# A warm-up of 128 instead of 256 rows, the sum of squares on VectorE and the cast of the scan on ScalarE, in an eight-core layer

## The chip, the cores and the metric

The kernel runs on the 8 cores of one Trainium2 chip (two dies of four cores). The metric is the device time of the slowest core in microseconds. Engine names in what follows: PE is TensorE, ACT is ScalarE, DVE is VectorE, POOL is GpSimd, SP is SyncE, which here only issues transfers.

## What is computed

```python
xn = _layernorm(x, axis=-1)                       # x: (4, 4096, 2048)
x = x + _L0_attn_ref(xn, ...) + _L0_ffn_ref(xn, ...)

# _L0_attn_ref
xp = jnp.einsum('btd,ed->bte', x, W_in)
dt = jax.nn.softplus(jnp.einsum('btd,hd->bth', xp, W_dt) + b_dt)
a = jnp.exp(dt[..., None] * A_cont)               # A_cont = -exp(log_A)
ys[t] = a[t] * ys[t - 1] + xh[t]                  # written as an associative scan
y = jnp.einsum('btd,ed->bte', ys.reshape(Bsz, Tlen, D), W_out)

# _L0_ffn_ref: weights int8, 2048 -> 8192 -> 2048
gate = jax.nn.silu(_qmatmul(x, w_gate, s_gate))
up = _qmatmul(x, w_up, s_up)
return _qmatmul(gate * up, w_down, s_down)
```

## The kernel before, in words

Each core takes 2048 consecutive rows of x (half a sequence of one batch). The scan would need the state of the rows before; instead every core begins WU = 256 rows early (zeros for the first half of a sequence) and lets the state decay in. So T = 2304 rows, 18 tiles of 128, are normalised and projected, and 2048 are put out. The rows are also cut into chunks of 512, 512, 512, 512 and 256 (CH_OFF, CH_LEN).

Nothing is scheduled by a planner: each engine and each queue runs its instructions in the order in which the Python emits them, and semaphores tie them together.

Start-up. emit_wc_step(r), 16 times, folds W_dt into W_in: a 1 MB piece of W_in is loaded by POOL (L219, cast to bf16 in the transfer), 16 matmuls of 32 columns (L226), an ACT copy (L231). Between the steps stand the first ten emit_ln_front and the first eight emit_ln_back.

emit_ln_front(tile): ACT issues the load of one x tile of 128x2048 f32 into one of three buffers xtb (L253), waits for it and squares it with a running sum (L259); DVE sums the tile (L265) and makes the small statistics (L267 to L274). emit_ln_back(tile): ACT takes the inverse root by Ln and Exp (L284, L287), the shift (L290), and writes the normalised tile in bf16 to xnb (L294); SP sends it to the scratch xn_scr (L300). From the fourth tile on, xnb is written only when the write of three tiles back has landed.

emit_tr(chunk): SP waits until all writes to xn_scr emitted so far have landed and issues 16 transposing transfers into xnT, 128x(chunk length) each (L317). emit_dtl(chunk): 16 matmuls give the dt logits of the chunk (L330), five ACT steps make the softplus (L337 to L346), three DVE steps split it in two bf16 parts (L348 to L354).

emit_m1_et(pass, et), one group for each of 16 feature tiles in each of two passes. Pass 0 covers chunks 0 and 1 (1024 columns), pass 1 chunks 2, 3 and 4 (1280 columns). In a group: the selector matmuls spread dt over the partitions (L402, L405), ACT takes the exponential into ab (L410), the projection takes 16 matmuls for each chunk (L424), ACT copies the result from PSUM to xpsb (L439), the DVE scan runs over the pass's columns (L451). Then emit_cast_spill of the group before: DVE casts the scan's result to bf16 (L470) and POOL writes it to ys_scr (L478). ab, xpsb, ysb and ybfb have two buffers each; the selector banks of pass 0 have one each.

In pass 0 the remaining tiles are normalised between the groups (dicts fr for fronts, bk for backs), and chunks 2, 3 and 4 are transposed behind groups 4, 8 and 10, their dt logits behind groups 5, 9 and 11:

```python
bk = {0: 8, 1: 9, 2: 10, 3: 11, 4: 12, 5: 13, 6: 14, 7: 15, 8: 16, 9: 17}
```

After pass 1 the feed-forward part runs: 64 steps of 128 matmuls of 512 columns (L611, gate and up), then four blocks of the down and output projections (L722, L728) with the residual added (L736). Its first loads wait until all of ys_scr is written.

Of the kernel before, what the change touches and what calls it, by code (L numbers as in the profile page):

```python
# [17 lines left out]
P = 128  # L18
# [4 lines left out]
WU = 256  # L23
# [3 lines left out]
CH_LEN = (512, 512, 512, 512, 256)  # L27
# [47 lines left out]
def build_nc():  # L75
# [24 lines left out]
    with contextlib.ExitStack() as top:  # L100
# [69 lines left out]
        xps_b = [AE(nc.sbuf_tensor(f"xpsb{i}", [P, 1280], F32)) for i in range(2)]  # L170
# [4 lines left out]
        a_b = [AE(nc.sbuf_tensor(f"ab{i}", [P, 1280], F32)) for i in range(2)]  # L175
# [3 lines left out]
        ys_b = [AE(nc.sbuf_tensor(f"ysb{i}", [P, 1280], F32)) for i in range(2)]  # L179
        ybf_b = [AE(nc.sbuf_tensor(f"ybfb{i}", [P, 1280], BF16)) for i in range(2)]  # L180
# [55 lines left out]
        PASS_LEN = (1024, 1280)  # L236
# [8 lines left out]
        def emit_ln_front():  # L245
# [10 lines left out]
            r_dx.wait(AC, kb)  # L256
            if i >= 3:
                AC.wait_ge(c_xn.h, i - 2)
            achain(AC.activation(out=xsq_s[:, :], in_=xt_b[kb][:, :], func=AF.Square,  # L259
                                 accum_out=stats[:, cb + 1:cb + 2]))  # L260
            sq_done = e_act.n
# [4 lines left out]
            VE.wait_ge(e_act.h, sq_done)  # L266
# [195 lines left out]
        def emit_cast_spill(p_of, gi2):  # L462
            k2 = gi2 % 2
            pln = PASS_LEN[0] if gi2 < NE else PASS_LEN[1]
            p2 = 0 if gi2 < NE else 1
            et2 = gi2 % NE
            VE.wait_ge(c_scan.h, gi2 + 1)
            if gi2 >= 2:
                VE.wait_ge(r_dys.h[k2], r_dys.cnt[k2])
            inst = VE.tensor_copy(out=ybf_b[k2][:, 0:pln], in_=ys_b[k2][:, 0:pln])  # L470
            c_ybf.inc(inst)
            GP.wait_ge(c_ybf.h, c_ybf.n)
            if p2 == 0:
                tt0, nblk, col0 = 0, 6, WU
            else:
                tt0, nblk, col0 = 6, 10, 0
            r_dys.refill(GP, k2)
            r_dys.inc(GP.dma_start(out=ys_scr[tt0:tt0 + nblk, :, et2, :]  # L478
                                   .rearrange("t p c -> p t c"),
                                   in_=ybf_b[k2][:, col0:col0 + nblk * P]  # L480
                                   .rearrange("p (t c) -> p t c", c=P)), k2)
# [17 lines left out]
        fr = {0: 1, 1: 1, 2: 1, 3: 1, 4: 1, 5: 1, 6: 1, 7: 1}  # L499
        bk = {0: 8, 1: 9, 2: 10, 3: 11, 4: 12, 5: 13, 6: 14, 7: 15, 8: 16, 9: 17}  # L500
# [326 lines left out]
```

## Time and profile before

| | us |
|---|---|
| median of 2 runs (3606.3 and 3607.96) | 3607.13 |
| the profiled execution | 3609.48 |
| its span, on core 0, the slowest | 3607.9 |
| span of core 3, the fastest | 3580.5 |
| spans of cores 1, 2, 4, 5, 6, 7 | 3584.4, 3592.2, 3601.9, 3592.8, 3606.7, 3589.5 |
| PE busy on core 0 | 3242.1 (90%) |
| DVE, ACT, POOL busy | 463.3, 537.8, 223.0 |
| mean granted TensorE clock on core 0 | 0.967 |

The span is the time from the first to the last instruction of one core; the profiled execution's own time includes a little around it. Busy times add up over stages that have different limits, so a stage is read from its own stretch: which engine works without a gap, what the others wait for, and what the chain of waits (the work followed back from the last instruction) passes through. The granted clock is TensorE's, 1.0 being 2.4 GHz and 0.5 being 1.2 GHz. A line with SPq or ACTq is a transfer's issue on that engine's queue.

### The profile page before, as it was taken

To read this page: it belongs to the slowest core of one execution; us is meant where nothing else is said; L and a number is where in the kernel's file an instruction comes from. 1 tells how busy PE (TensorE), PEld (TensorE's weight loads), DVE (VectorE), ACT (ScalarE), POOL (GpSimd) and SP (SyncE) were. 2 spreads that over 40 slices of the span, in tenths; PEclk is the share of its full clock that TensorE was granted. 3 is DMA by queue.
4 is the path that set the end of the run, shared out by engine and by line. 5 is a ranking of instruction groups with operands and counts; after the bars stand their busy time and mean duration, and the time that the engine had idled before them with its cause. 6 is when DMAs were issued, how large, how long until landed. Compare 5 with 4: busy or idle time off the path is not lost.

```text
span 3607.9 us, 36929 instructions; the slowest of 8 cores (3580.5 to 3607.9 us)
## 1 busy us (share of the span) xinstructions
PE 3242.1 (90%) x15088; PEld 1460.5 (40%) x15088; DVE 463.3 (13%) x540; ACT 537.8 (15%) x776; POOL 223.0 (6%) x318
## 2 busy tenths in 40 slices
PE   0164897999999999999999999979998997997999
PEld 0021343444444444444444444434433443443444
DVE  1132232000000000000000002200013004003000
ACT  2243222111211111112211111100000000000000
POOL 1000111000001000100010001000000000000000
PEclk9887898999999999999999999989999999998999
DMA  8755443112111211221121113256456547546443
GB/s 184 140 146 118 85 84 94 53 53 71 53 53 56 68 53 53 59 65 53 53 67 57 53 53 106 88 139 223 177 213 217 180 175 252 183 175 233 175 175 114
DMA packets 126758, 419.03 MB, mean 116 GB/s; under 512 B 51248, under 2 KB 51264, under 8 KB 111488
## 3 DMA queue, kind: packets, MB, share of 16 engines
q0 software_dynamic: 44544, 176.52, 18.9%
q1 hardware_dynamic: 79456, 221.28, 18.2%
q10 hardware_dynamic: 2592, 18.88, 1.7%
q8 instruction: 122, 2.00, 0.2%
q14 instruction: 44, 0.36, 0.0%
HBM read 322.38 MB, written 68.16 MB: 108 GB/s over the span
## 4 chain that ended last, share of the span: by engine, by line
PE 85%; DMA 8%; SPq 2%; ACT 2%; issue 1%; DVE 1%; POOL 0%; ACTq 0%; DVEq 0%; POOLq 0%
PE ps_g L611 25%; PE ps_u L611 25%; PE pso L728 24%; PE pso L722 6%; PE ps_xp L424 5%; DMA xtb<-x_full 4%; SPq L317 2%; DMA wdq_sb<-wd 2%; DVE wdq_sb L550 1%; ACT xsq_s L259 1%; DMA xn_scr<-xnb 1%; DMA ftb<-f_scr 0%; PE psdtl L330 0%; ACT ab L410 0%; PE psdtl L402 0%
## 5 line engine op out<-in xcount | busy, mean ns | idle before, releaser
L728 PE MATMUL pso<-wdq_sb,ftb 128*128 128x512 bf16 x4096 | 920.2, 385 | 61.6 <-DVE wdq_sb L550 61.6
L611 PE MATMUL ps_g<-xnT,wgb 128*128 128x512 bf16 x4096 | 897.4, 380 | 17.4 <-DMA wgb<-wg 17.4
L611 PE MATMUL ps_u<-xnT,wub 128*128 128x512 bf16 x4096 | 894.5, 379 | 0.0
L728 PEld LDWEIGHTS pso<-wdq_sb,ftb 128*128 128x128 bf16 x4096 | 403.2, 99 | 567.8 <-issue 99.5
L611 PEld LDWEIGHTS ps_g<-xnT,wgb 128*128 128x128 bf16 x4096 | 400.7, 98 | 503.5 <-issue 21.5
L611 PEld LDWEIGHTS ps_u<-xnT,wub 128*128 128x128 bf16 x4096 | 401.4, 98 | 482.6
L634 DVE TENSOR_TENSOR fb<-gb,ub 128x512 bf16<-128x512 bf16 x256 | 108.8, 425 | 1565.8 <-ACT ub L626 1565.8
L626 ACT ACTIVATE ub<-ps_u,su_c 128x512 bf16<-128x512 f32 x256 | 175.9, 687 | 708.2 <-PE ps_u L611 708.2
L623 ACT ACTIVATE gb<-ps_g,sg_c 128x512 bf16<-128x512 f32 x256 | 175.9, 687 | 704.2 <-PE ps_g L611 704.2
L424 PE MATMUL ps_xp<-xnT,winTb 128*128 128x512 bf16 (+1 forms) x1280 | 265.2, 368 | 0.0
L722 PE MATMUL pso<-wo_sb,ytb 128*128 128x512 bf16 x1024 | 233.5, 381 | 26.1 <-DMA ftb<-f_scr 26.1
L424 PEld LDWEIGHTS ps_xp<-xnT,winTb 128*128 128x128 bf16 x1280 | 125.3, 100 | 142.9 <-issue 29.4
L736 DVE TENSOR_TENSOR obb<-pso,xsb 128x512 f32<-128x512 f32 x64 | 44.2, 691 | 1049.0 <-PE pso L728 1049.0
L638 POOL DMA_DIRECT2D f_scr<-fb x64 | 75.9, 1185 | 1632.4 <-DVE fb L634 1581.3
L722 PEld LDWEIGHTS pso<-wo_sb,ytb 128*128 128x128 bf16 x1024 | 100.8, 98 | 149.3 <-issue 30.4
L550 DVE TENSOR_TENSOR wdq_sb<-wdq_sb,sdqb 128x4096 bf16<-128x4096 bf16 x32 | 140.2, 4421 | 96.6 <-DMA wdq_sb<-wd 96.5
L226 PE MATMUL psdtl<-wdtT_s,winNb 128*128 128x32 bf16 x256 | 9.4, 188 | 121.4 <-ACT wc_sb L231 96.4
L330 PE MATMUL psdtl<-xnT,wc_sb 128*32 128x512 bf16 (+1 forms) x80 | 24.0, 474 | 100.4 <-DMA xnT<-xn_scr 84.0
L544 POOL DMA_DIRECT2D wdq_sb<-wd x32 | 17.2, 537 | 776.5 <-PE pso L728 775.5
L265 DVE TENSOR_REDUCE stats<-xtb 128x1 f32<-128x2048 f32 x18 | 41.1, 2286 | 159.4 <-DMA xtb<-x_full 159.4
L451 DVE TENSOR_TENSOR_SCAN ysb<-ab,state_s,xpsb 128x1280 f32<-128x1280 f32 x16 | 46.1, 2884 | 103.6 <-ACT xpsb L439 103.6
L226 PEld LDWEIGHTS psdtl<-wdtT_s,winNb 128*128 128x128 bf16 x256 | 8.1, 104 | 122.5 <-issue 122.5
(57 smaller groups left out, 495.6 us busy)
## 6 DMA issues: line engine op xcount, KB each, us to landing
ftb<-f_scr SPq DMA_DIRECT2D x64, 2048.0 KB, 8.9
ytb<-ys_scr SPq DMA_DIRECT2D x64, 512.0 KB, 9.7
wgb<-wg POOLq DMA_DIRECT2D x64, 512.0 KB, 5.4
wub<-wu POOLq DMA_DIRECT2D x64, 512.0 KB, 6.2
f_scr<-fb POOLq DMA_DIRECT2D x64, 512.0 KB, 5.3
wdq_sb<-wd POOLq DMA_DIRECT2D x32, 1024.0 KB, 15.6
xtb<-x_full ACTq DMA_DIRECT2D x18, 1024.0 KB, 8.5
winTb<-winT POOLq DMA_DIRECT2D x32, 512.0 KB, 5.3
```

Source lines behind the costliest of these rows:

```text
L317: r_dtr.inc(SY.dma_start(out=xnT[:, dt * T + off: dt * T + off + ln], in_=xn_scr[off:off + ln, dt * P:(dt + 1) * P], transpose=True), kc)
L424: inst = TE.matmul(ps_xp6[:, bank * 512: bank * 512 + ln], winT_b[kw][:, dt * P:(dt + 1) * P], xnT[:, dt * T + off: dt * T + off + ln], st ...
L451: inst = VE.tensor_tensor_scan(out=ys_b[k2][:, 0:pln], data0=a_b[k2][:, 0:pln], data1=xps_b[k2][:, 0:pln], initial=init, op0=ALU.mult, op1 ...
L550: c_wds.inc(VE.tensor_tensor(out=wv, in0=wv, in1=sdq_b[q % 2][:, :].unsqueeze(1) .broadcast_to([P, GJ, QW]), op=ALU.mult))
L611: inst = TE.matmul(ps[:, cols], wsb[kb][:, dt * P:(dt + 1) * P], xnT[:, dt * T + WU + ch * 512: dt * T + WU + ch * 512 + 512], start=(dt = ...
L623: inst = AC.activation(out=g_b[kf2][:, cols], in_=ps_g[:, cols], func=AF.Silu, scale=sg_c[:, j:j + 1])
L626: inst = AC.activation(out=u_b[kf2][:, cols], in_=ps_u[:, cols], func=AF.Identity, scale=su_c[:, j:j + 1])
L634: c_f.inc(VE.tensor_mul(out=f_b[kf2][:, cols], in0=g_b[kf2][:, cols], in1=u_b[kf2][:, cols]))
L638: r_df.inc(GP.dma_start(out=f_scr[:, :, j, :].rearrange("t p c -> p t c"), in_=f_b[kf2][:, :].rearrange("p (t c) -> p t c", c=P)), kf2)
L722: inst = TE.matmul(ps_o[ko][:, :], yt_b[kf][:, dt * P:(dt + 1) * P], wo_sb[q % 2][:, dt * QW:(dt + 1) * QW], start=(dt == 0), stop=False)
L728: inst = TE.matmul(ps_o[ko][:, :], ft_b[kf][:, jt * P:(jt + 1) * P], wdq_sb[:, jt * QW:(jt + 1) * QW], start=False, stop=(jt == NJ - 1))
L736: c_add.inc(VE.tensor_add(out=ob_b[ko][:, :], in0=ps_o[ko][:, :], in1=xs_b[kf][:, :]))
```

## The change

WU becomes 128: T is 2176, 17 tiles, the last chunk has 128 rows, pass 1 has 1152 columns. The output blocks are split 7 and 9 between the passes instead of 6 and 10. The last front and the last back fall away. In emit_ln_front ACT only issues the load; the sum of squares is a DVE instruction (scalar_tensor_tensor with accum_out) behind the DVE sum, written to the same scratch xsq_s. In emit_cast_spill the cast is an ACT copy; the waits for the scan and for the spill of two groups back move to ACT with it.

```diff
--- before.py
+++ after.py
@@ -20,11 +20,11 @@
 NE = 16
 ND = 16
 NJ = 64
-WU = 256
+WU = 128
 TR = 2048
 T = WU + TR
 CH_OFF = (0, 512, 1024, 1536, 2048)
-CH_LEN = (512, 512, 512, 512, 256)
+CH_LEN = (512, 512, 512, 512, 128)
 NCH = 5
 NQ = 4
 QW = 512
@@ -167,17 +167,17 @@
         xt_b = [AE(nc.sbuf_tensor(f"xtb{i}", [P, DM], F32)) for i in range(3)]
         xn_b = [AE(nc.sbuf_tensor(f"xnb{i}", [P, DM], BF16)) for i in range(3)]
         xsq_s = AE(nc.sbuf_tensor("xsq_s", [P, DM], BF16))
-        xps_b = [AE(nc.sbuf_tensor(f"xpsb{i}", [P, 1280], F32)) for i in range(2)]
+        xps_b = [AE(nc.sbuf_tensor(f"xpsb{i}", [P, 1152], F32)) for i in range(2)]
         z_s = AE(nc.sbuf_tensor("z_s", [P, 512], F32))
         zl_s = AE(nc.sbuf_tensor("zl_s", [P, 512], F32))
         zr_s = AE(nc.sbuf_tensor("zr_s", [P, 512], F32))
         dt_b = [AE(nc.sbuf_tensor(f"dtb{i}", [P, 512], F32)) for i in range(2)]
-        a_b = [AE(nc.sbuf_tensor(f"ab{i}", [P, 1280], F32)) for i in range(2)]
+        a_b = [AE(nc.sbuf_tensor(f"ab{i}", [P, 1152], F32)) for i in range(2)]
         dthi_s = AE(nc.sbuf_tensor("dthi_s", [32, T], BF16))
         dtlo_s = AE(nc.sbuf_tensor("dtlo_s", [32, T], BF16))
         sel_sb = AE(nc.sbuf_tensor("sel_sb", [32, NE * P], BF16))
-        ys_b = [AE(nc.sbuf_tensor(f"ysb{i}", [P, 1280], F32)) for i in range(2)]
-        ybf_b = [AE(nc.sbuf_tensor(f"ybfb{i}", [P, 1280], BF16)) for i in range(2)]
+        ys_b = [AE(nc.sbuf_tensor(f"ysb{i}", [P, 1152], F32)) for i in range(2)]
+        ybf_b = [AE(nc.sbuf_tensor(f"ybfb{i}", [P, 1152], BF16)) for i in range(2)]
         state_s = AE(nc.sbuf_tensor("state_s", [P, NE], F32))
 
         wn_ctx = contextlib.ExitStack()
@@ -233,7 +233,7 @@
 
         PASS_CH = ((0, 1), (2, 3, 4))
         PASS_OFF = (0, 1024)
-        PASS_LEN = (1024, 1280)
+        PASS_LEN = (1024, 1152)
         wm_vals = {}
         pexp_at = {}
         exp_at = {}
@@ -253,17 +253,14 @@
             r_dx.inc(AC.dma_start(out=xt_b[kb][:, :],
                                   in_=x_full[row0:row0 + P, :]), kb)
             cb = 12 * (i % 3)
-            r_dx.wait(AC, kb)
-            if i >= 3:
-                AC.wait_ge(c_xn.h, i - 2)
-            achain(AC.activation(out=xsq_s[:, :], in_=xt_b[kb][:, :], func=AF.Square,
-                                 accum_out=stats[:, cb + 1:cb + 2]))
-            sq_done = e_act.n
             r_dx.wait(VE, kb)
             if i >= 3:
                 VE.wait_ge(c_xn.h, i - 2)
             vchain(VE.reduce_sum(out=stats[:, cb:cb + 1], in_=xt_b[kb][:, :], axis=AX))
-            VE.wait_ge(e_act.h, sq_done)
+            vchain(VE.scalar_tensor_tensor(out=xsq_s[:, :], in0=xt_b[kb][:, :],
+                                           scalar=1.0, in1=xt_b[kb][:, :],
+                                           op0=ALU.mult, op1=ALU.mult,
+                                           accum_out=stats[:, cb + 1:cb + 2]))
             vchain(VE.tensor_scalar_mul(out=stats[:, cb + 2:cb + 3],
                                         in0=stats[:, cb:cb + 1], scalar1=-INV_D))
             vchain(VE.tensor_scalar_mul(out=stats[:, cb + 3:cb + 4],
@@ -464,16 +461,17 @@
             pln = PASS_LEN[0] if gi2 < NE else PASS_LEN[1]
             p2 = 0 if gi2 < NE else 1
             et2 = gi2 % NE
-            VE.wait_ge(c_scan.h, gi2 + 1)
+            AC.wait_ge(c_scan.h, gi2 + 1)
             if gi2 >= 2:
-                VE.wait_ge(r_dys.h[k2], r_dys.cnt[k2])
-            inst = VE.tensor_copy(out=ybf_b[k2][:, 0:pln], in_=ys_b[k2][:, 0:pln])
+                AC.wait_ge(r_dys.h[k2], r_dys.cnt[k2])
+            inst = AC.activation(out=ybf_b[k2][:, 0:pln], in_=ys_b[k2][:, 0:pln],
+                                 func=AF.Copy)
             c_ybf.inc(inst)
             GP.wait_ge(c_ybf.h, c_ybf.n)
             if p2 == 0:
-                tt0, nblk, col0 = 0, 6, WU
+                tt0, nblk, col0 = 0, 7, WU
             else:
-                tt0, nblk, col0 = 6, 10, 0
+                tt0, nblk, col0 = 7, 9, 0
             r_dys.refill(GP, k2)
             r_dys.inc(GP.dma_start(out=ys_scr[tt0:tt0 + nblk, :, et2, :]
                                    .rearrange("t p c -> p t c"),
@@ -496,8 +494,8 @@
         wn_ctx.close()
         emit_winT_load(0)
         emit_winT_load(1)
-        fr = {0: 1, 1: 1, 2: 1, 3: 1, 4: 1, 5: 1, 6: 1, 7: 1}
-        bk = {0: 8, 1: 9, 2: 10, 3: 11, 4: 12, 5: 13, 6: 14, 7: 15, 8: 16, 9: 17}
+        fr = {0: 1, 1: 1, 2: 1, 3: 1, 4: 1, 5: 1, 6: 1}
+        bk = {0: 8, 1: 9, 2: 10, 3: 11, 4: 12, 5: 13, 6: 14, 7: 15, 8: 16}
         for et in range(NE):
             emit_m1_et(0, et)
             if et in bk:
```

ACT in pass 0, from the exponentials of group 2 on to those of the next. ab are the decay factors, xpsb the projection, xnb the normalised tile, xtb the x tile, ybfb the bf16 result of the scan. Before:

```order
L410 ACTIVATE ab<-ps_xp,negA_s 128x512 x2
L439 ACTIVATE xpsb<-ps_xp 128x1024
L284 ACTIVATE stats<-stats,eps_c 128x1
L287 ACTIVATE stats<-stats 128x1
L290 ACTIVATE stats<-stats 128x1
L294 ACTIVATE xnb<-xtb,stats 128x2048
L253 DMA xtb<-x_full 128x2048
L259 ACTIVATE xsq_s,stats<-xtb 128x2048
L410 ACTIVATE ab<-ps_xp,negA_s 128x512 x2
```

The change (its line numbers are its own):

```order
L407 ACTIVATE ab<-ps_xp,negA_s 128x512 x2
L436 ACTIVATE xpsb<-ps_xp 128x1024
L467 ACTIVATE ybfb<-ysb 128x1024
L281 ACTIVATE stats<-stats,eps_c 128x1
L284 ACTIVATE stats<-stats 128x1
L287 ACTIVATE stats<-stats 128x1
L291 ACTIVATE xnb<-xtb,stats 128x2048
L253 DMA xtb<-x_full 128x2048
L407 ACTIVATE ab<-ps_xp,negA_s 128x512 x2
L436 ACTIVATE xpsb<-ps_xp 128x1024
```

The square behind the load is gone, and the cast stands between the copy of the projection and the small steps of the next tile.

DVE at the same place, between two scans (printed as SCALAR_TENSOR_TENSOR ysb). Before:

```order
L451 SCALAR_TENSOR_TENSOR ysb<-ab,xpsb 128x1024
L459 COPY state_s<-ysb 128x1
L265 TENSOR_REDUCE stats<-xtb 128x1
L267 TENSOR_SCALAR stats<-stats 128x1
L269 TENSOR_SCALAR stats<-stats 128x1
L271 TENSOR_TENSOR stats<-stats 128x1
L274 TENSOR_TENSOR stats<-stats 128x1
L470 CAST ybfb<-ysb 128x1024
L451 SCALAR_TENSOR_TENSOR ysb<-ab,xpsb 128x1024
```

The change:

```order
L448 SCALAR_TENSOR_TENSOR ysb<-ab,xpsb 128x1024
L456 COPY state_s<-ysb 128x1
L259 TENSOR_REDUCE stats<-xtb 128x1
L260 SCALAR_TENSOR_TENSOR xsq_s,stats<-xtb 128x2048
L264 TENSOR_SCALAR stats<-stats 128x1
L266 TENSOR_SCALAR stats<-stats 128x1
L268 TENSOR_TENSOR stats<-stats 128x1
L271 TENSOR_TENSOR stats<-stats 128x1
L448 SCALAR_TENSOR_TENSOR ysb<-ab,xpsb 128x1024
```

The square (xsq_s) follows the sum of the tile; the cast no longer precedes the scan.

SP at the end of pass 0, from the transposes of chunk 2 to those of chunk 4. Before:

```order
L317 DMA_TRANSPOSE xnT<-xn_scr 128x512 x16
L300 DMA xn_scr<-xnb 128x2048 x4
L317 DMA_TRANSPOSE xnT<-xn_scr 128x512 x16
L300 DMA xn_scr<-xnb 128x2048
L317 DMA_TRANSPOSE xnT<-xn_scr 128x256 x16
```

The change:

```order
L314 DMA_TRANSPOSE xnT<-xn_scr 128x512 x16
L297 DMA xn_scr<-xnb 128x2048 x4
L314 DMA_TRANSPOSE xnT<-xn_scr 128x512 x16
L314 DMA_TRANSPOSE xnT<-xn_scr 128x128 x16
```

The write between the last two sets of transposes is gone, and the last set has 128 rows of x each.

## Rows read from the trace of the kernel before

**Rows 1.** Windows of core 0: PE, PEld, DVE, ACT, POOL busy, PEclk, DMA share, GB/s

```profile
0.00:187.00 187.00, 21.45 (x292) 12.33 (x292) 32.92 (x59) 53.24 (x81) 14.39 (x29) 0.94 0.79 156
187.00:425.00 238.00, 150.77 (x604) 60.01 (x604) 73.95 (x93) 86.41 (x118) 20.00 (x29) 0.80 0.55 124
425.00:612.00 187.00, 165.40 (x882) 82.08 (x880) 63.19 (x36) 45.11 (x65) 28.11 (x38) 0.96 0.42 84
612.00:3608.00 2996.00, 2904.49 (x13312) 1306.10 (x13312) 293.23 (x352) 353.03 (x513) 160.51 (x222) 0.98 0.35 115
```

**Rows 2.** The same view of the start-up alone

```profile
10.00:150.00 140.00, 12.22 (x263) 9.15 (x264) 26.37 (x46) 43.71 (x68) 10.10 (x19) 1.00 0.95 189
```

**Rows 3.** Timeline of the SP queue, 60 to 425 us: start us, us, line, out<-in

```profile
90.32 43.45 SPq L317 DMA_TRANSPOSE xnT<-xn_scr  x16
...
344.44 21.06 SPq L317 DMA_TRANSPOSE xnT<-xn_scr  x16
365.65 0.47 SPq L300 DMA_DIRECT2D xn_scr<-xnb  x1
369.27 21.14 SPq L317 DMA_TRANSPOSE xnT<-xn_scr  x16
```

**Rows 4.** Chain of waits, 140 to 620 us: start us, us, what

```profile
151.87 1.13 SPq L317
...
187.27 9.00 PE ps_xp L424 x32
...
250.57 2.10 ACT xnb L294
...
290.53 5.13 PE psdtl L330 x16
...
396.45 8.51 PE ps_xp L424 x32
405.92 7.01 PE ps_xp L424 x32
...
429.85 8.76 PE ps_xp L424 x48
...
585.59 8.76 PE ps_xp L424 x48
```

**Rows 5.** Timeline of ACT: start us, us, line, out<-in, idle before and its releaser

```profile
198.51 0.33 ACTq L253 DMA_DIRECT2D xtb<-x_full  x1
209.02 1.91 ACT L259 ACTIVATE xsq_s<-xtb 128x2048 bf16<-128x2048 f32 x1 [8.54 <-DMA xtb<-x_full]
...
212.32 1.02 ACT L439 ACTIVATE xpsb<-ps_xp 128x1024 f32<-128x1024 f32 x1
...
334.67 2.10 ACT L294 ACTIVATE xnb<-xtb,stats 128x2048 bf16<-128x2048 f32 x1
```

**Rows 6.** Tile xtb, 187 to 260 us: five loads from issue to landing

```profile
DMA to landing us min/median/max: 5.5/6.7/10.4
```

**Rows 7.** Timeline of PE, three places

```profile
17.20 0.59 PE L226 MATMUL psdtl<-wdtT_s,winNb 128*128 128x32 bf16 x16 [17.20 <-DMA winNb<-winN]
...
368.09 5.59 PE L330 MATMUL psdtl<-xnT,wc_sb 128*32 128x512 bf16 x16 [27.60 <-DMA xnT<-xn_scr]
...
391.80 2.83 PE L330 MATMUL psdtl<-xnT,wc_sb 128*32 128x256 bf16 x16 [2.16 <-DMA xnT<-xn_scr]
```

**Rows 8.** Groups by line and shape: busy us, mean ns, idle before

```profile
L451 DVE TENSOR_TENSOR_SCAN ysb<-ab,state_s,xpsb 128x1280 f32<-128x1280 f32 x16 | 46.1, 2884 | 103.6 <-ACT xpsb L439 103.6
...
L265 DVE TENSOR_REDUCE stats<-xtb 128x1 f32<-128x2048 f32 x18 | 41.1, 2286 | 159.4 <-DMA xtb<-x_full 159.4
...
L470 DVE CAST ybfb<-ysb 128x1280 bf16<-128x1280 f32 x16 | 13.2, 826 | 3.8 <-DVE ysb L451 3.8
...
L410 ACT ACTIVATE ab<-psdtl,negA_s 128x256 f32<-128x256 f32 x16 | 7.6, 473 | 122.2 <-PE psdtl L405 122.2
...
L271 DVE TENSOR_TENSOR stats<-stats 128x1 f32<-128x1 f32 x18 | 2.9, 159 | 1.9
```

## The prediction

> **What bounds the kernel now.** I read the windows first [rows 1]. From 612 us to the end the PE is busy 2904 of 2996 us at a mean granted clock of 0.98; the change does not touch an instruction there. Its whole field is the first 612 us, and no gain can pass that. There the PE is busy 21 of 187, 151 of 238 and 165 of 187 us, so the question is in each stretch who holds it.
>
> Start-up, to 187 us: the DMA share is 0.95 from 10 to 150 us [rows 2]. The transfers bound it, though ACT idles on them. The SP queue needs 43.45 us there to issue 16 transposes, against 21.06 later [rows 3]; the first chunk's transposes end at 133.8, the second's begin at 151.87, and the first projection matmul runs at 187.27 [rows 4].
>
> Pass 0, 187 to 425 us, DMA share 0.55, so latency and not bandwidth. ACT issues the load of an x tile and, as its next work, squares that tile: it issues at 198.51 and sits idle 8.54 us before the square at 209.02 [rows 5]. Behind the square stand the exponentials that free the banks for the PE. Then the chain is: normalised tile 12 (ACT L294 at 250.57), its write, 16 transposes, the dt matmuls at 290.53 [rows 4]; tile 16 at 334.67 [rows 5], transposes at 344.44 [rows 3], dt matmuls at 368.09 [rows 7]; tile 17's write at 365.65 and the last transposes from 369.27 [rows 3], dt matmuls at 391.80 [rows 7].
>
> Pass 1, from 429.85: groups of 48 matmuls follow each other to 585.59, 15 periods in 155.74, 10.38 us each, 8.76 of it the 48 matmuls [rows 4]. The PE is the bound.
>
> **The change, part by part.** T is 2176 instead of 2304, one x tile and 128 columns less; the square goes to DVE (and ACT no longer waits for the tile); the cast of the scan goes to ACT.
>
> The new DVE square is not in the trace. Nearest are the reduce over the same 128x2048, 2.29 us, and the two-source scan, 2.88 for 1280, that is 2.25 ns an element or 4.6 for 2048 [rows 8]. A cast-like rate (0.83 for 1280) would give 1.3. I take 2.3, since reduce reads the same f32 tile once per element; range 1.3 to 4.6. A tile then takes DVE 2.3 + 2.3 + four small operations (0.16 each, with hand-overs I estimate 1.1) = 5.7 us. The reduce row says 2.29 for 2048 f32 elements. The Trainium skill, "VectorE: DVE Perf Modes", section on the TRN2 errata, states for a two-source f32 operation (N + 151)/0.96 ns, 2.29 for 2048; by that rule the sum is mine, by the scan's rate it is the first rival's.
>
> (a) Start-up. ACT's waits go, but the transfers are the same ones; 140 us at 0.95 hold about 7 us of slack. The first chunk's transposes start when tile 3 is written, and that comes earlier, since tiles 1 to 3 no longer pass through an ACT that waits. Now 18.1 us lie between the end of the first transposes (133.8) and the second's start; what must follow is the writes of tiles 4 to 7, with tile 7's normalisation in them, since it needs the buffer that tile 4's write frees. One tile takes 9.8 us from its normalisation at 334.67 to the transposes at 344.44 [rows 5, 3]; four that overlap I estimate at 13. Bounds: nothing gained (transfers alone decide) and 13. I take 8.
>
> (b) M1(0) to the dt matmuls of chunk 2, now 187.27 to 290.53, of which 63.3 to tile 12's normalisation. Counted from M1(0): load 10 is issued at 11.2 as now. ACT goes on at once: exponentials, copy (1.02) when M1(1) ends (9.0 + 1 for the selectors + 7.0 = 17), cast 1.1 (ACT's 2048 take 2.10 [rows 5], half of it), the small normalising steps 1.1, load 11 at 20.4. Load 10 lands near 21.7 (209.02 − 198.51 after its issue); stats to 27.4; scan 1 to 29.9; ACT's cast 1 waits for it, then load 12 at 32.2. DVE has 5.7 + 2.3 (scan) + 0.3 = 8.3 us a tile; where a load (median 6.7 [rows 6]) is late, two tiles take 8.3 + 2.2 + 6.7 to 7.5, so 8.7 to 9 each. Tiles 10, 11, 12 thus pass ACT at 32, 41 and 50.3, instead of 63.3. Gain 13. The cover of the cast is ACT's idle time, and the price where DVE is late is in this sum: ACT waits in the cast, and behind it stand the small steps of the next tile, its load and the next exponentials, for which the PE waits. The cast's other wait, for the spill of two groups back, moves with it and is long met; POOL's spill behind it starts some us later, before a load of weights that is needed two groups on. DVE's scan stands behind the wait for the tile as it does now. Bounds: 18 (the PE's own 8 us a group, 9 + 4x8 + 4) and 5 (square 4.6, 10.8 us a tile). From tile 12 to the dt matmuls the 40.0 us of [rows 4] stay: write, transposes, landing.
>
> (c) To the dt matmuls of chunk 3, now 290.53 to 368.09. Tile 16's normalisation is at +44.1 today: three rounds of load 10, square, exponentials. Tile 16's load is issued at +16.6 (now tile 17's follows it; that one is gone), lands at +26.6, stats +32.4, scan 7 +34.9, cast +36, tile 16 at +37.2. Gain 7. From there 33.4 us stay. Bounds: 3 (square 4.6 and a late load) and 9.
>
> (d) The end of pass 0. With 17 tiles no write stands between the transposes: SP goes from the end of 344.44's 21.06 straight to the last 16. These took 21.14 for 256 rows of x against 21.06 for 512, so 128 rows are priced the same, 21. They start 3.7 us earlier, which removes the PE's wait of 2.16 before 391.80 [rows 7]; late next is the PE itself. The dt matmuls of 128 columns cost half of 2.83: 1.4. The group after that wait takes 8.51 instead of 7.01, the clock having dropped: 1.5 more if it stays up. Sum 5; bounds 3 (clock drops anyway) and 7 (the selector matmuls too).
>
> (e) Pass 1. 16 matmuls of 256 columns take 8.76 − 7.01 = 1.75, 0.109 each [rows 4], which is all columns; 128 columns then cost 0.056. The upper bound: 16 matmuls of 32 columns behind a full weight load took 0.59 less one latency, about 0.027 each [rows 7], so at most 0.027 of load would stay bare: 0.067 from 96 columns more, or, wholly serial, 0.08. Gain per group 0.86 (0.46 to 0.86). The two selector matmuls give 0.1 more, and the exponential between them and the next ones (0.47 for 256 columns [rows 8], 0 to 0.24 saved, I take 0.11). So 1.07 a group, period 9.3, 17 over 16 groups; bounds 10 and 18. ACT carries in a group the exponentials, the copy and now the cast of the group before, whose scan is 6 us old: about 4 of 9.3 us. It hides wholly; with that cover gone it would cost 1.1 a group. DVE is relieved of 0.83.
>
> (f) The end. Last copy −0.1, scan −0.3, cast on ACT 1.2 instead of 0.83, and its neighbour's spill is issued later, between the same two: zero, ±1. The down-projection sees the same blocks, only split 7 and 9 instead of 6 and 10: zero.
>
> Sum: 8 + 13 + 7 + 5 + 17 = 50 us. The profiled execution took 3609.5 for its span of 3607.9; it becomes 3559.5. It stood 2.4 above the median of the runs, 3607.1, from which I forecast 3557. A measurement of this kernel tells about 2% from no change, 72 us, so this is within it. The slowest core of the table is core 0, core 3 is 27 us ahead; all eight run the same stages, and I let the order stand.
>
> **Rivals.**
> First, the square runs at the scan's rate (4.6). For it: the scan is the only two-source f32 operation of that length here. Then (b) gives 5, (c) 3, (a) 8, (d) 5, (e) 17: 38, 3569.
>
> Second, transfers hold everything: more loads in flight at once make each slower, as at the start. For it: DMA share 0.95; against: 0.55 in pass 0. (a) 0, (b) 6, (c) 3, (d) 4, (e) 17: 30, 3577.
>
> Third, more falls: the transposes of chunk 0 get clear of the loads (43 us become nearer 21) and the rounds run at the PE's pace. (a) 18, (b) 18, (c) 9, (d) 7, (e) 18: 70, 3537. Against it: the loads are then in the same minutes.
>
> Fourth, slower than before: the square with its sum runs as two passes on DVE, scan-like and reduce-like, 4.6 + 2.3 = 6.9, and DVE becomes what all 17 tiles wait for. That is 4.6 more on each, 78, against my 50: 28 slower, 3635. It decides from 2.3 + 50/17 = 5.2 us for the square on. Against it: ACT's square with its sum is one pass of 1.91 [rows 5], and nothing in the rows runs on DVE at such a pace.
>
> **How the numbers follow.** Forecast 0.65; first rival 0.13, second 0.13, third 0.07, fourth 0.02. 3557 is the likeliest. The range of 80% goes from 3540, short of the third rival, to 3582, past the second, which stands on one core's rows. Faster by over 2% means under 3535, the third rival's upper tail: 0.04. Slower by over 2% means over 3679, 0.01. Within: 0.95.
>
> **What would show it.** DVE's square at 2.3 us; ACT idle before the next exponentials under 5 us in pass 0; normalised tile 12 some 50 us after the first projection matmul, tile 16 some 37 after chunk 2's dt matmuls; no idle before the last dt matmuls and the group behind them at 7.01; a period of 9.3 in pass 1; the gate matmuls from about 562 instead of 612, and 2996 us behind that. I am wrong if the square exceeds 4.6, if the second transposes do not start before 150, if the period stays above 9.7, or if the stretch after the first gate matmul changes by over 10 us.

## The result, and the profile after

The change takes 3558.48 us, the median of 7 runs, against 3608.12, the median of 6, for the kernel before in the same measurement. The ratio is 0.9861, with a 95% interval of 0.9849 to 0.9874: about 50 us faster. The forecast was 3557.

The slowest core of the profiled execution is now core 7, with 3560.9 us. Its windows answer to [rows 1]; the columns are the same.

```profile
0.00:174.00 174.00, 21.99 (x292) 12.49 (x292) 55.90 (x79) 34.11 (x61) 14.41 (x29) 0.92 0.80 168
174.00:393.00 219.00, 146.24 (x624) 60.02 (x624) 77.50 (x88) 81.05 (x113) 22.17 (x29) 0.82 0.57 128
393.00:560.00 167.00, 146.09 (x865) 69.84 (x864) 44.32 (x18) 60.36 (x83) 29.38 (x38) 0.95 0.48 92
560.00:3561.00 3001.00, 2906.24 (x13312) 1306.60 (x13310) 293.38 (x352) 354.25 (x513) 160.47 (x222) 0.98 0.36 115
```

The last line is the feed-forward part and the down-projection: 2906 of 3001 us busy at a granted clock of 0.98, as in [rows 1]. Everything that changed lies ahead of it. Compare the lengths of the three stretches ahead of it: 187, 238 and 187 us before, 174, 219 and 167 now.

One profile has eight cores, and they differ by up to 27 us. To see what a stage does, the beginnings of the stages were read from the PE's timeline of every core: the first projection matmul (L424 before, L421 now), the dt matmuls of chunks 2 and 3 (L330, L327), the first selector matmul of pass 1, the end of the last projection matmul, the first gate matmul. The table gives medians over the eight cores of one profiled execution of each kernel, each number the length of a stage in us. It includes the experiments e1 to e6, which are described below.

| kernel | start to first projection (latest core) | to dt of chunk 2 | to dt of chunk 3 | to pass 1 | pass 1 | to first gate matmul | from there |
|---|---|---|---|---|---|---|---|
| before | 177.2 (187.2) | 100.2 | 75.3 | 61.8 | 165.5 | 17.3 | 2996.1 |
| the change | 174.1 (175.0) | 86.1 | 68.6 | 60.7 | 148.7 | 17.5 | 2995.7 |
| e1, warm-up only | 174.6 (178.9) | 99.6 | 70.4 | 54.9 | 148.7 | 17.3 | 2997.1 |
| e2, square only | 174.4 (177.2) | 85.8 | 68.0 | 62.8 | 165.5 | 18.3 | 2997.3 |
| e3, cast only | 174.9 (187.6) | 102.0 | 76.4 | 63.0 | 165.5 | 18.5 | 2997.3 |
| e4, cast left on DVE | 173.5 (174.4) | 88.2 | 67.2 | 55.0 | 148.7 | 17.4 | 2995.6 |
| e5, dt matmuls late | 174.0 (176.7) | 96.1 | 38.4 | 27.1 | 151.0 | 18.0 | 2996.5 |
| e6, first transposes late | 175.1 (175.8) | 85.5 | 68.2 | 60.0 | 148.7 | 18.2 | 2999.3 |

Pass 1 hardly differs between cores (165.5 on each of them before, 148.7 after), the stages ahead of it by a few us. From the slowest core before (core 0) to the slowest now (core 7), 12.9 us fell away at the start, 15.8 to chunk 2, 7.6 to chunk 3, nothing to pass 1, 16.8 in it; 0.7 came back before the gate matmuls and 5.5 behind them, where core 7 is slower than core 0 was. Some executions of nearly every kernel here ran with the clock of one die below the other's and took longer; they are left out of all ratios and of the experiments' medians, and where a profile caught one (e7, e9) only its other die is read.

The chain of waits on core 7 answers to [rows 4]. Columns: start us, us, what.

```profile
174.38 9.21 PE ps_xp L421 x32
...
223.68 2.10 ACT xnb L291
...
261.84 6.40 PE psdtl L327 x16
...
299.86 2.11 ACT xnb L291
...
349.91 6.29 DMA xnT<-xn_scr
356.45 1.87 PE psdtl L327 x16
360.13 8.49 PE ps_xp L421 x32
369.58 7.01 PE ps_xp L421 x32
...
393.51 7.91 PE ps_xp L421 x48
...
533.27 7.91 PE ps_xp L421 x48
```

Tile 12 is normalised 49.3 us after the first projection matmul (223.68 − 174.38; before 63.3), the dt matmuls of chunk 2 come at 87.5 (before 103.3). Pass 1: 15 periods from 393.51 to 533.27 are 139.76, so 9.32 each, and 48 matmuls take 7.91.

Next the groups of the slowest core by line and shape, to [rows 8]. Columns: busy us, mean ns of one, idle before.

```profile
L448 DVE TENSOR_TENSOR_SCAN ysb<-ab,state_s,xpsb 128x1152 f32<-128x1152 f32 x16 | 41.9, 2617 | 107.3 <-ACT xpsb L436 107.3
L260 DVE SCALAR_TENSOR_TENSOR xsq_s<-xtb 128x2048 bf16<-128x2048 f32 x17 | 39.0, 2292 | 1.8
L259 DVE TENSOR_REDUCE stats<-xtb 128x1 f32<-128x2048 f32 x17 | 38.9, 2286 | 95.8 <-DMA xtb<-x_full 95.1 <-DVE state_s L456 0.6
...
L467 ACT ACTIVATE ybfb<-ysb 128x1152 bf16<-128x1152 f32 x16 | 18.6, 1165 | 1.9 <-DVE ysb L448 1.9
...
L407 ACT ACTIVATE ab<-psdtl,negA_s 128x128 f32<-128x128 f32 x16 | 5.9, 370 | 91.7 <-PE psdtl L402 91.7
```

The new square (L260) takes 2.29 us, as the reduce does. The cast of 1152 columns on ACT takes 1.17, where DVE took 0.83 for 1280. The small exponential takes 0.37 instead of 0.47.

### The profile page after: what moved, and what is told of

Same layout as the page of the kernel before. It is cut to its first block, busy times and chain, and to the rows that moved or that the text cites. A ratio compares the mean times of both kernels' runs of the same rounds, so it can differ in the third digit from the quotient of the medians.

```text
span 3560.9 us, 36849 instructions; the slowest of 8 cores (3541.2 to 3560.9 us)
## 1 busy us (share of the span) xinstructions
PE 3220.6 (90%) x15088; PEld 1449.0 (41%) x15088; DVE 471.1 (13%) x537; ACT 529.8 (15%) x768; POOL 226.4 (6%) x318
## 3 DMA queue, kind: packets, MB, share of 16 engines
q1 hardware_dynamic: 77264, 220.23, 18.3%
## 4 chain that ended last, share of the span: by engine, by line
PE 85%; DMA 6%; SPq 3%; DVE 2%; issue 1%; ACT 1%; POOL 0%; DVEq 0%; ACTq 0%; POOLq 0%
PE ps_g L609 25%; PE ps_u L609 25%; PE pso L726 24%; PE pso L720 6%; PE ps_xp L421 5%; SPq L314 3%; DMA wdq_sb<-wd 2%; DMA xtb<-x_full 1%; DMA xn_scr<-xnb 1%; DVE wdq_sb L548 1%; DMA ftb<-f_scr 1%; DMA winNb<-winN 0%; PE psdtl L327 0%; DVE xsq_s L260 0%; DVE stats L259 0%
## 5 line engine op out<-in xcount | busy, mean ns | idle before, releaser
L609 PE MATMUL ps_g<-xnT,wgb 128*128 128x512 bf16 x4096 | 896.9, 380 | 18.2 <-DMA wgb<-wg 18.2
L421 PE MATMUL ps_xp<-xnT,winTb 128*128 128x512 bf16 (+1 forms) x1280 | 244.5, 351 | 0.0
L421 PEld LDWEIGHTS ps_xp<-xnT,winTb 128*128 128x128 bf16 x1280 | 114.0, 98 | 134.3 <-issue 19.3
L327 PE MATMUL psdtl<-xnT,wc_sb 128*32 128x512 bf16 (+1 forms) x80 | 24.9, 494 | 127.7 <-DMA xnT<-xn_scr 95.0
L327 PEld LDWEIGHTS psdtl<-xnT,wc_sb 128*32 128x32 bf16 x80 | 9.6, 132 | 142.8 <-issue 141.3
L448 DVE TENSOR_TENSOR_SCAN ysb<-ab,state_s,xpsb 128x1152 f32<-128x1152 f32 x16 | 41.9, 2617 | 107.3 <-ACT xpsb L436 107.3
L476 POOL DMA_DIRECT2D ys_scr<-ybfb x32 | 32.1, 1002 | 315.8 <-ACT ybfb L467 300.6
```

The lines of the kernel that those rows point to most:

```text
L421: inst = TE.matmul(ps_xp6[:, bank * 512: bank * 512 + ln], winT_b[kw][:, dt * P:(dt + 1) * P], xnT[:, dt * T + off: dt * T + off + ln], st ...
L448: inst = VE.tensor_tensor_scan(out=ys_b[k2][:, 0:pln], data0=a_b[k2][:, 0:pln], data1=xps_b[k2][:, 0:pln], initial=init, op0=ALU.mult, op1 ...
L609: inst = TE.matmul(ps[:, cols], wsb[kb][:, dt * P:(dt + 1) * P], xnT[:, dt * T + WU + ch * 512: dt * T + WU + ch * 512 + 512], start=(dt = ...
```

## Where the rounds of pass 0 went

ACT on core 0, from its timeline, to be read against [rows 5]:

```profile
203.90 1.06 ACT L467 ACTIVATE ybfb<-ysb 128x1024 bf16<-128x1024 f32 x1 [2.14 <-DVE ysb L448]
...
206.10 0.33 ACTq L253 DMA_DIRECT2D xtb<-x_full  x1
...
212.96 1.06 ACT L467 ACTIVATE ybfb<-ysb 128x1024 bf16<-128x1024 f32 x1 [2.82 <-DVE ysb L448]
...
215.15 0.33 ACTq L253 DMA_DIRECT2D xtb<-x_full  x1
```

A load is issued at 206.10, the next at 215.15: 9.05 us apart. ACT no longer idles for a tile (8.54 us at 209.02 before), but it does idle before the cast, 2.14 and 2.82 us, and what ends that is DVE's scan. DVE over the same time:

```profile
204.70 2.29 DVE L259 TENSOR_REDUCE stats<-xtb 128x1 f32<-128x2048 f32 x1 [0.63 <-DVE state_s L456]
207.09 2.29 DVE L260 SCALAR_TENSOR_TENSOR xsq_s<-xtb 128x2048 bf16<-128x2048 f32 x1
...
210.52 2.29 DVE L448 TENSOR_TENSOR_SCAN ysb<-ab,xpsb 128x1024 f32<-128x1024 f32 x1
...
213.31 2.29 DVE L259 TENSOR_REDUCE stats<-xtb 128x1 f32<-128x2048 f32 x1 [0.24 <-DVE state_s L456]
...
231.44 2.29 DVE L259 TENSOR_REDUCE stats<-xtb 128x1 f32<-128x2048 f32 x1 [1.15 <-DMA xtb<-x_full]
```

Sum, square, small steps, scan, and the next sum begins 8.61 us after the last one. The idle time in front of it is 0.24 us, the hand-over. So up to tile 12, which is summed at 213.31, DVE is the engine that is waited for, and hardly waits itself. The last two rounds with a load take 9.52 and 9.37 us: there DVE waits for the x tile again, 1.15 and 1.00 us.

## Experiments

All of them start from the kernel before or from the change; no output is left out in any.

### The three parts alone: e1, e2, e3, and the change without the cast: e4

e1 is the first part of the diff (WU, chunk lengths, buffers, 7 and 9 blocks, fr and bk), with the square on ACT and the cast on DVE as before:

```diff
-WU = 256
+WU = 128
-CH_LEN = (512, 512, 512, 512, 256)
+CH_LEN = (512, 512, 512, 512, 128)
```

> The shorter warm-up alone; square on ACT and cast on DVE as before. Sum of the parts (mine): pass 1 gives 17 us (period 9.3 instead of 10.38), the write of tile 17 that stood between the last two sets of transposes gives 3 to 4, the start-up and the rounds of pass 0 stay as they were: about 20 faster, ratio 0.994 to 0.995. Rival (the one tile less also unblocks ACT in pass 0 and carries most of the gain): 35 or more faster, ratio under 0.990.

Measured: 3576.16 us, ratio 0.9913 (0.9893 to 0.9932). That is 31 us by the ratio, between my 20 and the rival's 35. Pass 1 gave the 16.8 that were expected. The stage to chunk 3 gave 4.9, which I had given to the square alone, and the stage to pass 1 gave 6.9 where I had written 3 to 4.

e2 is the square alone:

```diff
-            achain(AC.activation(out=xsq_s[:, :], in_=xt_b[kb][:, :], func=AF.Square,
-                                 accum_out=stats[:, cb + 1:cb + 2]))
+            vchain(VE.scalar_tensor_tensor(out=xsq_s[:, :], in0=xt_b[kb][:, :],
+                                           scalar=1.0, in1=xt_b[kb][:, :],
+                                           op0=ALU.mult, op1=ALU.mult,
+                                           accum_out=stats[:, cb + 1:cb + 2]))
```

> Only the sum of squares moved to DVE, warm-up 256 and cast on DVE as before. Mine: ACT no longer waits for the tile it has just sent for; from the first projection matmul to chunk 2's dt matmuls 103 us become about 88 (tiles pass at 9 to 9.5 us), to chunk 3's 77 become 71 to 73, the start loses up to 12 on the cores that were slow in it and nothing on the fast ones; pass 1 stays at 10.38: 25 to 33 faster, ratio 0.991 to 0.993. Rival (transfers bound both stages, so the wait only moves from ACT to DVE): under 10 faster, ratio over 0.997.

Only two executions count, 3588.03 and 3589.03, so there is no interval. Those of the kernel before in that measurement lie between 3606.7 and 3618.8. That is about 22 us faster, a little short of my 25 to 33, and by its profile 14.4 to chunk 2 and 7.3 to chunk 3. The rival (transfers bind both stages) falls: it had the stage to chunk 2 unchanged.

e1 and e2 both shorten the stage to chunk 3, by 4.9 and 7.3, and the change with both by 6.7. Two parts that each remove the same wait do not add. In the kernel before, ACT waits there for tile 17 ahead of the normalisation of tile 16 at 334.67 (ACT's timeline, core 0); e1 does not load that tile and in e2 ACT does not wait for it:

```profile
329.28 1.91 ACT L259 ACTIVATE xsq_s<-xtb 128x2048 bf16<-128x2048 f32 x1 [5.67 <-DMA xtb<-x_full]
```

e3 is the cast alone, e4 the change with this line back on DVE:

```diff
-            inst = VE.tensor_copy(out=ybf_b[k2][:, 0:pln], in_=ys_b[k2][:, 0:pln])
+            inst = AC.activation(out=ybf_b[k2][:, 0:pln], in_=ys_b[k2][:, 0:pln],
+                                 func=AF.Copy)
```

> Only the cast moved to ACT. Mine: before the change ACT is what the rounds of pass 0 wait for, and the cast of 1.05 us stands on it ahead of each load, so the eight rounds with a tile become 1 us longer each: 5 to 10 slower over pass 0, pass 1 unchanged at 10.38, the end of pass 1 to the first gate matmul 0.5 to 1 longer; ratio 1.0015 to 1.003. Rival (the cast is hidden, or frees DVE): 0 to 3 faster.

Measured: 3611.9 us, ratio 1.0001 (0.9987 to 1.0016). The stages of pass 0 are 1.8, 1.1 and 1.2 longer in the medians, the start was 2.3 shorter, though nothing in it was changed. My 5 to 10 was not found: the interval reaches to 5.8 slower at most.

> The whole change but with the cast left on DVE. Mine: DVE is what the rounds of pass 0 wait for in the change (8.6 us each), and the cast of 0.69 and its hand-over lengthen them by 0.5 to 0.9: 2 to 5 slower there; against it POOL's spill goes out earlier and no longer meets the last transposes, whose landing becomes 2.5 to 3 us instead of 5 to 7, so 3 to 4 faster there, and 0.8 at the end of pass 1. Together within 3 of the change, ratio to before 0.985 to 0.987. Rival (the cast's place does not matter to the last transposes): their landing stays at 5 to 7 us.

Measured: 3560.31 us, ratio 0.9864 (0.9845 to 0.9883), against 0.9861 for the change: the cast as a whole is worth nothing that can be measured. Inside, two effects stand against each other as expected. To chunk 2's dt matmuls e4 takes 88.2 instead of 86.1. To pass 1 it takes 55.0 instead of 60.7, and e1, which also has the cast on DVE, takes 54.9.

That last difference is the step at which my prediction failed, so here are its lines. First the change, core 7: POOL's issues near the last transposes, and the PE's matmuls that wait for them (timelines), then SP up to 362 us.

```profile
348.10 0.98 POOL L476 DMA_DIRECT2D ys_scr<-ybfb  x1 [40.95 <-ACT ybfb L467]
349.08 0.57 POOL L367 DMA_DIRECT2D winTb<-winT  x1
```

```profile
356.45 1.87 PE L327 MATMUL psdtl<-xnT,wc_sb 128*32 128x128 bf16 x16 [3.12 <-DMA xnT<-xn_scr]
```

```profile
81.60 43.41 SPq L314 DMA_TRANSPOSE xnT<-xn_scr  x16
125.16 6.01 SPq L297 DMA_DIRECT2D xn_scr<-xnb  x4
138.50 20.20 SPq L314 DMA_TRANSPOSE xnT<-xn_scr  x16
...
309.53 41.59 SPq L314 DMA_TRANSPOSE xnT<-xn_scr  x32
```

The 32 transposes from 309.53 to 351.1 stand without a write between them, as forecast. But the spill goes out at 348.10 and the load of the next weights right behind it, in the last 3 us of the issue. By the chain above, the last transpose then takes 6.29 us to land; the PE waits 3.12 before 356.45, and its next group takes 8.49 instead of 7.01. Now e4, core 7: POOL, and the same matmuls.

```profile
336.31 0.98 POOL L475 DMA_DIRECT2D ys_scr<-ybfb  x1 [40.47 <-DVE ybfb L467]
338.02 0.57 POOL L367 DMA_DIRECT2D winTb<-winT  x1 [0.73 <-PE ps_xp L402]
342.64 0.98 POOL L475 DMA_DIRECT2D ys_scr<-ybfb  x1 [4.05 <-DVE ybfb L467]
345.75 0.56 POOL L367 DMA_DIRECT2D winTb<-winT  x1 [2.12 <-PE ps_xp L421]
```

```profile
345.07 1.07 PE L327 MATMUL psdtl<-xnT,wc_sb 128*32 128x128 bf16 x16
```

This core is some 9 us ahead of core 7 of the change, so times must be counted from the issue of the last transpose, 341.1 here and 349.9 there. In the change the spill stands 1.8 us before it and the weights 0.8; in e4 the spill stands 4.8 and the weights 3.0 before it, and the next pair comes 1.6 and 4.7 behind. The transpose lands 3.47 us after its issue instead of 6.29, the dt matmuls at 345.07 have no idle time before them and take 1.07 us instead of 1.87.

All eight cores of each profile, counted in the same way (us):

| | before | the change | e4 | e1 |
|---|---|---|---|---|
| nearest weights issued, from the last transpose's issue | 0.0 to 1.2 | -1.7 to 0.6 | -3.7 to -2.7 | -4.6 to -2.5 |
| last transpose, issue to landing | 2.4 to 2.9 on four cores, 5.4 to 5.8 on four | 5.1 to 7.0 | 3.2 to 4.3 | 2.5 to 4.9 |
| PE's wait before chunk 4's dt matmuls | 2.1 to 6.4 | 0.8 to 3.1 | 0 to 1.1 | 0 to 1.1 |
| dt of chunk 3 to dt of chunk 4, median | 25.7 | 24.6 | 22.1 | 22.0 |
| from there to pass 1, median | 35.5 | 36.1 | 32.9 | 32.9 |

So the 5.7 us between the change and e4 have two parts: 2.5 us ahead of the last dt matmuls, and 3.2 behind them. The second part is the clock: on core 7 of the change the granted clock is 0.72 from 356.4 to 368.5 and 1.00 behind that. Cores 3 and 5 of the change waited only 0.81 us, kept 1.00 and took 32.9 like e4.

That the landing is late because of POOL's transfers is read from these rows and was not tried by itself. Of the two transfers the rows point to the weights more than to the spill. In the kernel before all eight cores have a spill 2.0 to 3.1 us ahead of the last transpose; the four with the weights at 0.0 to 0.9 us behind it land in 5.4 to 5.8, the four with the weights at 1.0 to 1.2 in 2.4 to 2.9. I had expected a landing of 2.5 to 3 in e4 and a gain of 3 to 4 there; the landing is slower and the gain larger.

### Does SP's order hold the start? e6

In the change the normalisation of tile 7 waits for the write of tile 4, which stands behind the first transposes on SP. ACT's timeline on core 0:

```profile
129.35 2.09 ACT L291 ACTIVATE xnb<-xtb,stats 128x2048 bf16<-128x2048 f32 x1 [27.80 <-DMA xn_scr<-xnb]
```

```diff
-            if r == 10:
-                emit_tr(0)
+        emit_tr(0)
         emit_tr(1)
```

> The change, with the transposes of chunk 0 emitted behind the start-up loop, so behind the writes of tiles 4 to 7 on SP. Mine: the start-up of the change is held by SP, which stands in slow transposes for 43 us while the normalisation of tile 7 waits 27.8 us for the write of tile 4; with the writes ahead, both sets of transposes run unloaded at 21 us each from about 109 on and the second ends near 151 instead of 159: first projection matmul at about 166 instead of 174, 6 to 10 faster than the change, ratio to before 0.983 to 0.985. Rival (the sum of all transfers bounds the start, in whatever order): first projection matmul within 2 us of 174 or later.

Measured: 3560.8 us, ratio 0.9868 (0.9814 to 0.9923); the first projection matmul at 175.1 in the median, 174.1 in the change. SP on core 0:

```profile
39.22 66.35 SPq L297 DMA_DIRECT2D xn_scr<-xnb  x8
117.88 41.63 SPq L314 DMA_TRANSPOSE xnT<-xn_scr  x32
```

The eight writes are out by 105.6, as I expected, but the transposes begin at 117.88, since the last write takes 12 us to land, among the loads. From there both sets run at 20.8 us each, to 159.5; in the change SP's second set on core 0 ends at 159.2. So the 27.8 us of waiting cost nothing. From 82 to 118 us the DMA share is about 1 in both orders (0.97 in the change, 1.01 in e6); to 138.5 it is 0.70 in the change, which still has writes and loads to move, and 0.43 in e6, where transposes stand alone, and both end within 0.3 us of each other. The rival holds, and my reading of the wait falls.

### Is DVE the bound of the rounds? e7

```diff
+            vchain(VE.scalar_tensor_tensor(out=xsq_s[:, :], in0=xt_b[kb][:, :],
+                                           scalar=1.0, in1=xt_b[kb][:, :],
+                                           op0=ALU.mult, op1=ALU.mult,
+                                           accum_out=stats[:, cb + 1:cb + 2]))
```

> The change, with the sum of squares on DVE done twice (the same result): 2.4 us more DVE work for each of 17 tiles. Mine: DVE sets the rounds of pass 0 (8.6 us each in the change), so these become 11 us: to chunk 2's dt matmuls 8 to 10 more, to chunk 3's 2.4 more, the start 0 to 3 more (tile latency, transfers hide the rest), nothing elsewhere: 10 to 15 slower than the change. Rival (the loads set the rounds, DVE waits for them anyway): under 4 slower.

> The change with the sum of squares done twice on DVE, once more, for a profile with both dies undisturbed. The first profile's undisturbed die had 5 us more from the first projection matmul to chunk 2's dt matmuls and 9 more in the span. Mine: the same again, 8 to 12 slower than the change in all. Rival: under 4.

In the first run no execution counts; on cores 4 to 7 of its profile the stage to chunk 2's dt matmuls took 4.5 us more than on the same cores of the change (medians 91.2 and 86.7). In the second run one execution counts, 3569.42 us, 11 more than the change's 3558.48. In its profile the die of cores 0 to 3 took 92.3 us to chunk 2's dt matmuls (median), against 86.0 on the same cores of the change: 6.3 more. Three tiles, 10 to 12, are worked on in that stage ahead of them, with 7.2 us of added work. To chunk 3 it was 0.9 more, at the start 1.6. DVE on core 0:

```profile
204.69 2.29 DVE L259 TENSOR_REDUCE stats<-xtb 128x1 f32<-128x2048 f32 x1 [0.24 <-DVE state_s L460]
...
215.70 2.29 DVE L259 TENSOR_REDUCE stats<-xtb 128x1 f32<-128x2048 f32 x1 [0.24 <-DVE state_s L460]
```

The rounds take 11.01 us instead of 8.61, as expected, and DVE's idle time in front of the sum stays at 0.24. DVE bounds these rounds. My 8 to 10 for the whole stage was too high, and of the 2.4 expected to chunk 3 only 0.9 showed; why was not looked into.

### What still holds pass 0: e5, e8, e9, e10

The PE's waits on core 7 of the change, from 170 to 395 us (columns: sum in us, count, longest):

```profile
PE psdtl L327 <- DMA xnT<-xn_scr: 70.6, 3, 35.8
```

It waits 70.6 us for transposes before three sets of dt matmuls, whose results only pass 1 needs. e5 emits these later:

```diff
-            elif et == 5:
-                emit_dtl(2)
...
-            elif et == 9:
-                emit_dtl(3)
+            elif et == 9:
+                emit_dtl(2)
...
-            elif et == 11:
-                emit_dtl(4)
+            elif et == 13:
+                emit_dtl(3)
+            elif et == 15:
+                emit_dtl(4)
```

> The change, with the dt matmuls of chunks 2, 3 and 4 emitted behind groups 9, 13 and 15 of pass 0 instead of 5, 9 and 11 (only pass 1 needs them). Mine: what is left of pass 0 is the PE standing in its own order before dt matmuls whose transposes are not there (33 and 30 us on core 7); with groups to run meanwhile, pass 0 becomes 16 groups at 8 to 9 us and some 6 us for the last dt chain: from the first projection matmul to pass 1 about 150 us instead of 218, so 60 to 70 faster than the change, ratio to before 0.967 to 0.970. Rival (SP's queue of writes and transposes is the bound of pass 0, the PE only meets it later): 48 transposes and nine writes at about 1.25 to 7 us keep chunk 4 away until some 190 us, so 25 to 35 faster than the change, ratio 0.976 to 0.979.

Measured: 3514.26 us, ratio to before 0.974 (0.9697 to 0.9782). By the medians pass 0 fell from 215.4 to 161.6 us, 54 less, and pass 1 rose by 2.3. In time that is 44 faster than the change, by the medians and by the ratios (single executions 3509.78 to 3517.93), between mine and the rival. The PE's waits on its slowest core, core 4, and SP there:

```profile
PE psdtl L327 <- DMA xnT<-xn_scr: 8.8, 2, 5.7
PE ps_xp L399 <- ACT ab L407: 6.3, 4, 2.8
PE ps_xp L399 <- DVE dtlo_s L351: 6.0, 1, 6.0
PE psdtl L399 <- DVE dtlo_s L351: 3.5, 1, 3.5
```

```profile
190.27 39.05 SPq L297 DMA_DIRECT2D xn_scr<-xnb  x5
239.93 29.52 SPq L314 DMA_TRANSPOSE xnT<-xn_scr  x16
269.60 9.04 SPq L297 DMA_DIRECT2D xn_scr<-xnb  x4
281.73 48.31 SPq L314 DMA_TRANSPOSE xnT<-xn_scr  x32
```

The first set of transposes takes 29.52 us among the loads, the other two 48.31, and on this core the last ones are there 3 us after the PE has run out of groups (on the eight cores 0 to 3.3). Both theories hold in part: most of the 70 us was order alone; what is left are waits for transposes, which SP issues one set behind the other.

e8 is e5 and e6 together.

> e5 and e6 together. Mine: they act in different stretches, so the gains add: 66 to 80 faster than the change, ratio to before 0.964 to 0.968. Rival (an earlier first group only waits longer for the last transposes): no better than e5 alone.

Measured: 3515.31 us, ratio 0.9742 (0.9701 to 0.9783), no better than e5, as e6 by itself already said. The rival holds.

e9 is e5 with each set of transposes one group earlier (dt matmuls behind groups 8, 12 and 15); e10 the same with the cast on DVE.

> The change with late dt matmuls (behind groups 8, 12 and 15) and each set of transposes one group earlier (behind 3, 7 and 9 instead of 4, 8 and 10), so that it no longer waits for a tile that its chunk does not hold. Mine: in the run with late dt matmuls SP's chain of writes and transposes ended 3 us after the PE had run out of groups, and the last dt chain cost another 3.5; the chain now ends some 8 us earlier, so 3 to 7 faster than that run (about 3507 to 3511), ratio to before 0.971 to 0.973. Rival (the rounds of DVE alone now set pass 0): within 2 of it.

> The same with the cast on DVE. Mine: with the PE no longer held by the last transposes the collision of the spill costs nothing, and the cast only lengthens DVE's rounds: 0 to 4 slower than the same with the cast on ACT. Rival (the cast on ACT also holds the tiles back by making ACT wait for the scan): 2 or more faster.

e9: two executions count, 3509.32 and 3521.56, ratio 0.9737 (0.9701 to 0.9773): the same as e5, without the 3 to 7 that I had expected. The wait before the last dt matmuls did go (0 on cores 0 to 3 of its profile), but the stage to chunk 2 took 90.2 to 110.0 us on these cores (e5: 94.3 to 98.3), and the earlier transposes of chunk 2 took SP 34.5 to 57.0 us (e5: 29.3 to 31.3). e10: 3525.38 to 3539.66, ratio 0.9789 (0.9758 to 0.9819), some 19 us slower than e9 by the ratios, outside both of my expectations, though e9 has only two executions. The PE's waits in e10, core 2, and SP there:

```profile
PE ps_xp L421 <- DMA winTb<-winT: 19.7, 4, 10.6
PE psdtl L327 <- DMA xnT<-xn_scr: 17.8, 2, 12.3
```

```profile
219.32 51.92 SPq L314 DMA_TRANSPOSE xnT<-xn_scr  x16
```

A new wait has come in: the PE stands 19.7 us before projection matmuls for the weights winTb. In e10 all eight cores have it (6.3 to 25.2 us), in e9 two of the four that are read (6.6 and 8.8), in e5 none. The weights are loaded by POOL, in one queue with the spills. On core 2 those issued during the set of 51.92 us take 9.5 to 19.6 us to land, those ahead of it 5.0 to 10.8. Why the cast's place adds to it was not separated further. e5 is the version to keep: it beats both kernels.

## Why the prediction was right, and where it was not

The time (3557 for 3558.5) came out closer than the steps did. By the medians over the cores and by the slowest core:

(a) Start-up: 8, with 0 to 13. The slowest cores give 12.9, the medians 3.1. On the slowest the steps are those of the prediction: the first transposes start 8.7 us earlier (81.60 for 90.32) and take as long (43.41), and 13.5 us lie between the two sets instead of 18.1, where 13 was estimated. The price is missing in it: with the square on ACT the first set takes 36.6 to 37.6 us on the median core (before, e1, e3), with it on DVE 43.4 to 43.8 (the change, e2, e4, e5). It starts earlier and is slower, so the median core gains almost nothing; e1 and e3, whose start-up is that of the kernel before, stand at 174.6 and 174.9 too, so of the 3.1 only 0.5 to 0.8 stand out from what single profiles differ by. What is left is on the slow cores: with the square on ACT the latest core starts at 187.2, 178.9 and 187.6, with it on DVE, over five profiles, between 174.4 and 177.2 (183.2 in both profiles of e7, with the square twice). Why the slow ones lose their delay was not tested; e6 shows that the order of SP is not what decides it.

(b) To chunk 2: 13. Medians 14.1, slowest core 15.8. Load, stats, scan and cast went as laid out: rounds of 8.6 to 9.05 to tile 12 (forecast 8.7 to 9), tile 12 at 49.3 (50.3). The square cost 2.29 and 0.08 for reading the sum.

(c) To chunk 3: 7. Medians 6.7, tile 16 at +38.0 (299.86 − 261.84; forecast 37.2). Right in size; but the share of the square and that of the dropped tile overlap, which I had not seen.

(d) The end of pass 0: 5, measured 1.1. This is the step that failed, at "which removes the PE's wait of 2.16" and "late next is the PE itself", and with it the sentence in (b) by which POOL's later spill has no price. The write between the transposes is gone, but the 3.7 us are spent on the landing of the last transpose, which the sum left at what core 0 had before, 2.39, and which is 5.1 to 7.0 in the change. The PE still waits (3.12 on core 7), and the clock falls as before: 8.49 for the group, not 7.01. With the cast on DVE the wait is gone (e4: 55.0 for 61.8, 6.8 of gain, even more than I had summed); moving the cast gives 5.7 of it back (60.7 against 55.0), by the rows through POOL's weights and spill, which go out against the last transposes. The row of core 0 was also a mild one: in the same profile four cores waited 2.1 to 2.6 us before these matmuls and four 5.3 to 6.4.

(e) Pass 1: 17, measured 16.8. The 16 matmuls of 128 columns take 7.91 − 7.01 = 0.90, 0.056 each, the lower bound of my row and the rate of columns alone; no time for the weight loads shows beside it.

(f) The end: 0, measured 0.2 longer. The rest of the kernel: 2996.1 and 2995.7.

The medians add up to 42, the slowest cores to 47, the runs to 50. That 50 was met within a microsecond or two is luck in part: (d) was 4 too high, and (a) was 5 too high for the median core and 5 too low for the one that sets the time. (b), (c) and (e), 37 of the 50, were right in mechanism and size.

The rival with the scan's rate falls by the row of the square, 2.292 us, and the fourth rival with it. The Trainium skill, "VectorE: DVE Perf Modes", section on the TRN2 errata, gives (N + 151)/0.96 ns for the f32 tensor_tensor add, 2.29 us at 2048; the trace agrees for this instruction too.

## What to carry to other kernels

An engine that issues a load and works on it next turns the load's latency into a bound for all that is queued behind it; moving the work to another engine moved the bound there, and the rounds became as long as that engine's own work. A move that looks free by busy time can still change when a third queue issues its transfers, so ask what they will meet, and on every core, not only on the slowest. And look at what the PE waits for in its own order: three sets of matmuls that only the next pass needed held it for 70 us, and emitting them later gave nearly as much as the whole change.

## What was not expected of the hardware

The 16 transposes of 128 rows of x take SP as long as those of 512: they are issued 1.24 and 1.27 us apart, and a set takes 20 to 21 us when little else runs. Among loads of x and weights the same set took 23.3 to 45.0 in the change and up to 57.0 in e9. The landing of the last one varied from 2.4 to 7.0 us; it was 5.1 to 7.0 on every core of the change, where POOL issued weights from 1.7 us before it to 0.6 behind it, and 2.5 to 4.9 in e1 and e4, where they went out 2.5 to 4.6 us before. The dt matmuls of 512 columns that follow a wait took 4.9 to 6.5 us, the first of them 0.43 us apart and the later ones 0.22; for those of chunks 1 to 3 in the change the granted clock over the set is 0.55 to 0.73, so part of them ran at 1.2 GHz. In e5 those of chunk 3 took 3.6 on six cores, at a granted clock of 1.00, with 0 to 1.6 us of waiting before them.
